# SyncE's program ahead of the layers written out in straight lines, with constants for addresses and wait values

## What is computed

```python
h = relu(layernorm(x)); x = x + L0(h)   # edge features: h[src]*(1+coef*w), linear, relu; segment max over dst and src
h = relu(layernorm(x)); x = x + L1(h)   # four graph convolutions, each with a norm over the whole graph
h = relu(layernorm(x)); x = x + L2(h)   # weighted neighbour sum by src, linear, relu
h = relu(layernorm(x)); x = x + L3(...) # per node: sum, max and mean of 32 edge attributes, two linear layers
```

## Time and profile before

| | us |
|---|---|
| median of 3 runs | 14,810.56 |
| profiled execution | 14,776.96 |
| its span, first to last instruction | 14,775.2 |
| PE matmul busy | 8,251.6 (56%) |
| DVE, ACT, POOL busy | 5,889.9, 5,765.9, 5,862.9 (40%, 39%, 40%) |
| first and last gather of pass 1 (L660) | 95.2, 2,638.6 |
| first and last scatter of pass 2 (L690) | 2,817.1, 5,840.4 |
| first and last load wait of pass 3 (L532) | 6,030.2, 7,071.1 |
| first and last load wait of the attribute pass (L443) | 7,880.0, 9,813.4 |

### The profile page before, as it was taken

The page is one execution under the profiler, slowest core; times in us unless marked ns, Lnnn a source line. Parts: engine busy times, 40 slices in busy tenths (PEclk is TensorE's granted clock), DMA queues, the critical chain, the costliest instruction groups (busy, mean ns, idle before and its releaser), DMA issues. The chain is left out here.

```text
span 14775.2 us, 234540 instructions
## 1 busy us (share of the span) xinstructions
PE 8251.6 (56%) x68487; PEld 5775.3 (39%) x68487; DVE 5889.9 (40%) x10294; ACT 5765.9 (39%) x8522; POOL 5862.9 (40%) x5419
## 2 busy tenths in 40 slices
PE   3333333355555554107200003539999999997799
PEld 2222222245555453005100003435655566555455
DVE  5555555344444443105211003434444443444344
ACT  1111111133333332004100002228888888885677
POOL 5887887555555555560677771020000000000000
PEclk6555555566666666556555555669999999998999
DMA  4444444222222224519200104547767677673899
GB/s 136 140 142 143 142 137 144 61 63 66 64 65 64 64 64 53 45 31 258 53 0 14 20 20 104 137 103 200 206 188 205 188 206 205 187 205 112 153 171 163
DMA packets 2836522, 1744.01 MB, mean 118 GB/s; under 512 B 1859990, under 2 KB 2689020, under 8 KB 2835924
## 3 DMA queue, kind: packets, MB, share of 16 engines
q1 hardware_dynamic: 2509508, 1305.01, 36.6%
q10 hardware_dynamic: 153360, 277.67, 5.1%
q0 software_dynamic: 173184, 154.24, 4.8%
HBM read 1065.41 MB, written 502.11 MB: 106 GB/s over the span
## 5 line engine op out<-in xcount | busy, mean ns | idle before, releaser
L1072 PE MATMUL PS<-AG,T 128*64 128x512 bf16 (+1 forms) x22064 | 2558.5, 354 | 60.2 <-DVE RT L2047 26.9
L660 POOL DMA_INDIRECT G<-node_table,IDX x1664 | 2038.4, 1225 | 600.8 <-issue 590.7
L690 POOL DMA_INDIRECT records<-RT,IDX x1664 | 1690.0, 1016 | 1358.0 <-ACT RT L1326 853.8
L2021 DVE CAST AG<-AG 128x1792 bf16<-128x1792 uint8 x1176 | 1285.8, 1094 | 2006.3 <-PE PS L1072 1572.7
L1451 ACT CAST AG<-AG 128x1792 bf16<-128x1792 uint8 x1176 | 1968.4, 1683 | 219.7 <-DMA AG<-adj 106.7
L726 POOL DMA_INDIRECT adj<-OH,EA x1664 | 1725.8, 1037 | 671.5 <-issue 576.4
L1072 PEld LDWEIGHTS PS<-AG,T 128*64 128x64 bf16 x22064 | 1232.9, 110 | 934.1 <-ACT AG L1541 51.9
L1072 PE MATMUL PS<-AG,RT 128*64 128x512 bf16 (+1 forms) x11032 | 1506.7, 353 | 0.5 <-issue 0.3
L1451 ACT CAST M<-AG 128x1792 bf16<-128x1792 uint8 x588 | 990.7, 1685 | 284.0 <-PE PS L1072 241.9
L755 POOL DMA_INDIRECT AG<-node_table,srow x28 | 32.6, 1166 | 2680.8 <-issue 2680.8
L953 PE MATMUL PS<-R 98*128 98x128 f32 x3328 | 999.5, 394 | 0.0
(11 more groups left out here) (365 smaller groups left out, 13937.2 us busy)
## 6 DMA issues: line engine op xcount, KB each, us to landing
AG<-adj SPq DMA_DIRECT2D x2940, 224.0 KB
adj<-Z ACTq DMA_DIRECT2D x105, 1568.0 KB
G<-records SPq DMA_DIRECT2D x624, 128.0 KB
M<-same_dst SPq DMA_DIRECT2D x416, 128.0 KB
fill_rows<-Z ACTq DMA_DIRECT2D x104, 512.0 KB
runs_l<-R SPq DMA_DIRECT2D x208, 256.0 KB
G<-fill_rows SPq DMA_DIRECT2D x208, 256.0 KB
runs<-R ACTq DMA_DIRECT2D x208, 256.0 KB
```

The source lines that it names most:

```text
L660: pool.indirect_dma_start(G[:, i, q * D:(q + 1) * D], None, table, bass.IndirectOffsetOnAxis(ap=IDX[:, i, q:q + 1], axis=0)).then_inc(sem( ...
L690: pool.indirect_dma_start(rec, bass.IndirectOffsetOnAxis(ap=IDX[:, i, q:q + 1], axis=0), RT[:, i, q, :], None).then_inc(sem(f"scattered{i} ...
L1072: m = pe.matmul(PS[h * D:(h + 1) * D, base + c:base + c + w], stat(t), rhs[:, h * QW + c:h * QW + c + w], start=start and t == 0, stop=sto ...
L2021: dve.tensor_copy(RING[i], RAW[i]).then_inc(sem("conv_d"), 1)
```

## The change

SP's loops ahead of the layers (`gather_pass`, `step2`, `step3`, `attr_step`) are Python loops in place of loops of the program, so that each DMA and each wait stands in the program once for every time that it runs, with a constant address and a constant value. The counting of `turns` goes from all of SP's helpers, also from those of the layers (`adj_in`, `group_end`), whose loops stay. DMAs, their order, the awaited semaphores and the values are the same. The other engines' programs are unchanged.

```diff
             def runs_out(dst, c, i, n):
                 sp.wait_ge(sem("r_ready"), n + 1)
-                sp.sem_inc(sem("turns"), 1)
...
             def attr_out(d, x):
                 sp.wait_ge(sem("e_ready"), d + 1)
-                sp.sem_inc(sem("turns"), 1)
...
                 if positive(d - 1):
                     sp.wait_ge(sem("e_scanned"), d * 2 - 2)
-                sp.sem_inc(sem("turns"), 1)
                 for h in range(2):
...
                 for i in range(4):
                     step(0, i, "first")
-                with sp.Fori(1, NIT) as it:
+                for it in range(1, NIT):
                     for i in range(4):
                         step(it, i, "mid")
...
             for i in range(4):
                 step2(0, i, True)
-            with sp.Fori(1, NIT) as it:
+            for it in range(1, NIT):
                 for i in range(4):
                     step2(it, i, False)
...
                 if not first:
                     sp.wait_ge(sem("fwd3"), c - 3)
-                    sp.sem_inc(sem("turns"), 1)
...
             for i in range(4):
                 step3(0, i, True)
-            with sp.Fori(1, NIT) as it:
+            for it in range(1, NIT):
                 for i in range(4):
                     step3(it, i, False)
...
             attr_step(0, 0)
             attr_step(1, 1)
-            with sp.Fori(1, NCH // 2 - 1) as u:
+            for u in range(1, NCH // 2 - 1):
                 for x in range(2):
                     attr_step(u * 2 + x, x)
...
                 else:
                     sp.wait_ge(sem("conv_d"), u * (ND * NK) + (r * ND + (i // 2 + 1)))
-                sp.sem_inc(sem("turns"), 1)
                 sp.dma_start(RAW[i], adj[bass.ds(r * (NR * P) + i * P, P), bass.ds(g * (2 * QW), 2 * QW)])\
```

## The result

| | before | after |
|---|---|---|
| median, us | 14,814.24 (14,802.09 to 14,845.96, 4 runs) | 14,645.9 (14,625.96 to 14,660.22, 4 runs) |
| ratio | | 0.9879, interval 0.9866 to 0.9891 |
| profiled span | 14,775.2 | 14,658.4 |
| instructions in the profile, all / SP's | 234,540 / 29,857 | 222,153 / 17,470 |

The kernel became faster by 1.2%, some 170 us, where the forecast was 100. By the ratio, 14,810.56 turns into 14,631, just under the lower end of 14,640.

A forecast was written before the change was run, and what follows sets the result against it. SP's block was taken to bound only the attribute pass's fast part; POOL, PE or DMA bound most elsewhere. Gains 92 (attribute pass) + 5 (pass 3) + 2 (pass 1 and 2) = 99 us took 14,810.56 to 14,710, range 14,640 to 14,800.

The forecast's parts named there:

- main mechanism: Attribute pass, fast part: SP's block of five DMAs is on the path, and constants remove its register operations.
- Attribute pass, size: Attribute pass, fast part: 92 us gained, with 0 and 118 as ends.
- 118 us of the earlier trace: Attribute pass, fast part: upper end, 1.35 us per pair of chunks over 87.5 pairs, if all is passed on.
- 26 us given back by slower landing: Attribute pass, fast part: loads land later as DMA share rises by 0.09, 0.3 us per pair, 26 us in all.
- The block: Attribute pass, fast part: SP's five DMAs with gaps and a wait take 2.4 us against 3.65.
- Pass 1, 2 us forecast: Pass 1 goes at POOL's pace; with pass 2, at most the 9.8 us of index waits go, taken as 2.
- Slow parts: Pass 3 and attribute pass beside POOL's single-byte scatter: PE's own slowed pace, 1.38 us per instruction, sets them; gain nothing.
- One sign: Profile after, slow parts: 0.7 us instructions on SP would still be there.
- Pass 3, 5 us forecast: Pass 3, fast part: DMA engines are full, so most only queues; 5 us, with 0 and 26 as ends.
- the slow parts are SP's: Rival, chance 0.07: SP bounds the slow parts, saving 188 us in the attribute pass and 67 in pass 3; 14,455.
- the fast part is held by something else: Rival, chance 0.15: DMA landing or DVE's scans hold it, so loads land no earlier; 14,790 to 14,810.
- a straight line costs fetches: Rival, chance 0.08: fetching 3,120 straight-line DMAs costs time, a loss above 0.071 us per DMA; 14,865 at twice POOL's price.

The follow-up runs named there:

- e3: Before with only the attribute pass's loop of SP written out, without its counting of turns: 14,691.77, ratio 0.9927.
- e1: The kernel before, unchanged, profiled once more: 14,797.18.
- e2: The changed kernel once more with more rounds: 14,627.71, ratio 0.9881.
- e9: The kernel before once more, on a chip of the 12,480 kind: 12,462.92.
- e10: The kernel after once more, on a chip of the 12,480 kind: 12,433.11 against 12,470.06, ratio 0.9968.
- e5: Before with pass 1 alone straight and without its turns: 12,439.96 against 12,480.49, ratio 0.9961.
- e11: After with eight idle semaphore increments ahead of every DMA of SP's in pass 1: 12,464.62, ratio 0.9994.
- e13: After with DVE's scan in pass 1 put behind both groups of one-hots: 14,506.19 against 14,777.59, ratio 0.9816.
- e14: Before, with its loops, with DVE's scan in pass 1 put behind both groups of one-hots: 14,828.59, ratio 1.0041.
- e16: After with DVE's scan last in pass 1 and a wait at every 32nd adjacency scatter: 12,484.5 against 12,515.49, ratio 0.9976.
- e17: After with DVE's scan last in pass 1 and a wait at every eighth adjacency scatter: 12,821.39, ratio 1.0238.
- e18: Before, with loops and DVE's scan last in pass 1, run again on the other kind of chip: 12,347.97 (one execution) against 12,515.49.
- e15: After with POOL waiting at every eighth adjacency scatter until all before have landed: 13,784.6 (one execution) against 14,777.59.

## Why the prediction was right or wrong

*Direction and main mechanism: right.* The fast part of the attribute pass was limited by SP's block on the path, and the block shrank with the register operations. e3 alone gives 107 us.

*Attribute pass, size: 92 us forecast, 99 (before to after) and 110 (e1 to e2) measured.* The 118 us of the earlier trace rows were right as a ceiling. The mean pair lost 1.2 us (9.7 to 8.6, and the same from e9 to e10), where the forecast had 1.35 less 0.3 given back. Two terms were wrong and partly cancelled, which is luck. The 26 us given back by slower landing were worked out from the landing time of pass 3: that took two stages with different loads as points of one line, and the landing did not slow at all (2.65 to 2.58 us). The block was misjudged the other way, 2.4 us forecast and 2.72 measured, because the sum took a load's 0.38 us beside register work, and the single first load of the earlier trace rows, as its price in a straight line; there the loads of one line take 0.51 and 0.59, and four in a row 2.31 us as against 2.38. The shown pair took the 8.7 to 9.1 us that were forecast (8.85). The second window of a pair had less slack than was said: in before its transposes waited for its own load as well (0.35 us at 9313.29).

*Pass 1, 2 us forecast, some 45 measured: the step that put the result out of the range.* It read POOL's waits and took POOL's own pace as given. But a gather's duration is no constant (0.94 to 3.03 us in one pass), and what sets it is how it meets DVE's scan and one-hots. e5 shows the gain alone (41 us), e11 takes most of it away by pace, and in e13 and e14, without the meeting, straight lines gain nothing over loops (e16 and e17 even lose 31 us to e18). Shown are thus that SP's pace changes pass 1's length, that the whole change lies in the gathers' durations, and that the long gathers go with the meeting. What leads from SP's pace to the meeting stays open. By the profile before, the row to look at would have been the gathers' mean of 1,225 ns beside their median of 947.

*Slow parts, nothing forecast, nothing found: right.* 72 matmuls in 200 us and 33.7 us a chunk in every run on that kind of chip but e15, also where the attribute pass is straight and SP's block is under 4 us. One sign came only in part: of SP's five DMAs there the first four issue at their usual pace (0.36 to 0.59 us, where before they took 0.7 to 1.4), and only the last one still shows 0.7 us at times. The reason given, PE's own slowed pace, stands, and e15 shows that it goes with the scatter that does not wait.

*Pass 3, 5 us forecast:* 174 scans in 464.3 us before and in 462.7 after, 2 us, with the DMA share at 1.06 and 1.07. *Pass 2, layers, turns:* nothing, within the spread from profile to profile (pass 2 took 3,023 us before and 3,038 after, but 3,016 in both e1 and e2, and 3,004 to 3,054 in all on this kind).

*The rivals.* That the slow parts are SP's fell with the 72. That the fast part is held by something else fell with the earlier trace rows against the pair above, for the first kind of chip; on the other kind it is, in effect, what happens, by the scatter. That a straight line costs fetches: the instruction queues moved 74 packets before and 96 after, and no stretch became longer for it; of the 0.071 us per DMA nothing is to be seen. The Trainium skill (Runtime: NRT & Kernel Launch, Instruction fetch mechanics) lets a taken branch stall where its target has left the window. In before the branch (L563, 9304.35, 0.05 us) is followed by SP's next instruction 0.24 us after it ends, once per pair, where the median gap between SP's instructions is 0.05, so a stall is 0.2 us at most. That the body of so short a loop ever leaves the window, no row shows.

## What to carry to other kernels

Before an engine's pace is taken as given, look at the spread of its instructions' durations: where the mean is nearly a third over the minimum (1,225 ns over 940), something on another engine decides, and a change that only moves that engine in time has a price or a gain there. Cost SP's loop by the starts of its DMAs, and look where the register operations stand: behind a wait and a branch they were worth 0.86 us a block here, between loads in a row 0.07. And ask where a stage's end is hidden: some 100 us less in the attribute pass were worth all on one chip, and 118 less were worth nothing on another, where POOL's scatter ended later.

## What was not expected of the hardware

- The same program takes 14,800 us on some chips and 12,490 on others. Pass 2 takes 3,016 us and 2,131 (e1, e9), and beside the adjacency scatter a chunk of the attribute pass takes 33.7 and 4.8. The layers take the same to about 1% (4,769 and 4,825).
- On the slower kind, scatters of one byte that GpSimd issues without waiting slow the other engines' instructions too, and waiting for their landing at every eighth saved some 815 us net (13,784.6 against the 14,600 that after would take there, an estimate from e15's before, 14,777.59, and the ratio 0.988). On the faster kind the same waits cost some 436.
- A gather issued by GpSimd that starts in the same 20 ns as VectorE's one-hots behind a scan is in two cases of three (666 of 1,003) held through all four of them, 3.03 us for 0.94; gathers that start at other moments take 0.94 to 1.91. The Trainium skill (SBUF — State Buffer, SBUF: two separate sides) says that the two engines share a port pair that is locked for a whole instruction; the trace agrees in that the gathers lengthen, but the hold lasts over a run of four instructions (2.22 us together), not one.
